# Four edits to an eight-image, four-layer kernel on one core: stores from two queues, an input sum by rows, a constant from DRAM, a longer loop body

## The chip, the core and the metric

One core of a Trainium2 chip. The time is the device time of one execution in microseconds (us). Eight images of 16 channels and 128 x 128 pixels in float32 go through four layers; the 128 partitions hold image and channel, 16,384 columns the pixels.

## What is computed

Each layer adds to x its function of the group-normed x (`_gn`: mean and variance over pairs of channels). Cut to what matters:

```python
x = x + L0(gn(x))   # attention over the 3 rows of a 3x3 patch, 48 features, 4 heads, MLP with gelu; sum, 1x1 convolution, bias
x = x + L1(gn(x))   # out1 = mean, out3 = max over the image; out = W4 (x (1 + sigmoid(tanh(wh)) + sigmoid(tanh(gray))))
x = x + L2(gn(x))   # sum over 3x3 taps and channels of P/Q, P = polynomial of degree 5, Q = 1 + |polynomial of degree 4|
x = x + L3(gn(x))   # 3x3 convolution of silu(x) and of 8 cubic splines of x, bias
```

## The kernel before

The four layers run one after the other, each in blocks in which every engine has its own stream of instructions, with semaphores between them. A block ends when all streams have ended.

**Layer 0** (`layer0`) works in 64 chunks (`NCHUNKS`), each 8 image columns of 2 images. A round `n` runs four stages for four chunks: centring of chunk n, the heads of chunk n - 1, the attention of chunk n - 2, the MLP of chunk n - 3. `steps` (lines 179 to 187) gives each engine its rounds: the first 3 written out, then a loop `Fori` of (63 - 3) / 4 = 15 passes with a body of `TURNS` = 4 rounds, then the last 4 written out. PE, VectorE, ScalarE and GpSimd use it; SyncE's stream is written out whole. In each round ScalarE takes one exponential of the softmax (line 693).

**Layer 1** (`layer1`) loads x and the eight pieces of layer 0's result x1, which lies by columns (w outer, h inner). VectorE adds x, x1 and a bias piece by piece (line 827, a piece is 16 image columns) and takes four bn_stats of it (line 99); the semaphore `x_in[j]` says that a piece is there, `xb_in` that x and the bias are. After `Norm` come the maximum of each partition over the whole image (line 835), the folding of weights, and a loop of 16 tiles of 1024 columns (tanh gates). The result goes to `x2` in four stores, and normed and with edges of zeros to the tile `GP` (16,797 columns).

**Powers** (`powers`) takes `GP` in 21 chunks of 800 columns (the last 797). ScalarE and VectorE make the powers 1 to 5, and of each a high, a middle and a low part in bf16 (`hi`, `mid`, `lo`, three buffers each). SyncE stores each part of a chunk to `pw` in DRAM, 1000 KB a store, in runs of 1600 bytes; before ScalarE writes `hi` and VectorE `lo` of chunk k, they wait until the stores of chunk k - 3 have landed:

```python
if k >= BUF:
    act.wait_ge(stored[u], k // BUF * STORES)
```

After chunk 1 SyncE also loads the weights `wst` (9 loads).

**Layer 2** (`layer2`) reads `pw` in 33 x 2 = 66 pieces of 2036 columns ("supertiles"), each by 24 loads of 20 rows into one of three slots of `mv`. Three rows of `mv` are ones; VectorE sets all of `mv` to 1.0 slot by slot before the first loads (line 1328), and SyncE loads slot g after memset g + 1 (line 1184). TensorE waits for `c_in` (the small matrices `sums` and `pick`, loaded first of all) and for the 24 loads of a slot, then multiplies. Every other engine works on what TensorE makes.

**Layer 3** (`layer3`) is not touched. It has the only transfers that GpSimd issues before the change: loads `l_s<-g` of 64 partitions (lines 1619 to 1623).

In the traces, buffer prefixes are cut: `l_x` is X of layer 1, `l_g` G or GP of layer 1, `l_mv` is `mv`.

Of the kernel before, what the change touches and what calls it, by code (L numbers as in the profile page):

```python
# [11 lines left out]
P = 128  # L12
# [6 lines left out]
PW = W + 1  # L19
# [21 lines left out]
WCOLS = (NCG * (len(AROUND) // 2) + NCG) * 128  # L41
RAW2 = (CG * DEG + 1) * 2 * WCOLS // 128
# [105 lines left out]
SLOTS0 = 2  # L148
BANK = 512
# [7 lines left out]
assert FS == 64 and 2 * HREST == P and SETS * FS == P and (LEAD_OUT - LEAD_IN) % TURNS == 0  # L157
# [561 lines left out]
def layer1(nc, x, x1, bias0, x2, pair, w1, raw2, pieces, wst, pw):  # L719
# [7 lines left out]
    with ExitStack() as ctx:  # L727
# [4 lines left out]
        with ExitStack() as ctx1:  # L732
# [14 lines left out]
            top = sb1("l1_top", [P, 8])  # L747
            stat = sb1("l1_stat", [P, 8])
# [12 lines left out]
            xb_in = sem("l1_xb_in")  # L761
# [8 lines left out]
            sum_done = sem("l1_sum_done")  # L770
# [4 lines left out]
            padded = sem("l1_padded")  # L775
# [5 lines left out]
            with nc.Block() as block:  # L781
                @block.sync
                def _(sp):
                    sp.dma_start(rest2[:], raw2).then_inc(raw_in, 16)
                    for k in range(LOADS):
                        n = HW // LOADS
                        if k == 0:
                            sp.dma_start(X[:], x).then_inc(xb_in, 16)
                            sp.dma_start(shift0[:], bias0).then_inc(xb_in, 16)
                        sp.dma_start(G[:, k * n:(k + 1) * n], x1[:, k * n:(k + 1) * n]).then_inc(x_in[k], 16)  # L790
# [12 lines left out]
                    sp.wait_ge(stored, 7 * 16)  # L803

                @block.vector
                def _(dve):
# [11 lines left out]
                    image, laid = X[:].rearrange("p (h w) -> p w h", w=W), G.rearrange("p (w h) -> p w h", h=H)  # L818

                    def chunk_in(e, k):  # L820
                        if k % (norm.CHUNKS // LOADS) == 0:
                            j = k // (norm.CHUNKS // LOADS)
                            at = slice(j * cols, (j + 1) * cols)
                            e.wait_ge(x_in[j], 16)
                            if j == 0:
                                e.wait_ge(xb_in, 32)
                            link(v.scalar_tensor_tensor(image[:, at, :], laid[:, at, :], shift0[:], image[:, at, :], ALU.add, ALU.add))

                    def chunk(k, n):
                        at = k * n // H  # L830
                        return image[:, at:at + n // H, :]
# [3 lines left out]
                    link(v.reduce_max(top[:, 0:1], X[:], AX.X))  # L835
# [19 lines left out]
                    for t in range(NT + 2):  # L855
# [4 lines left out]
                        if 1 <= t <= NT:  # L860
                            j = (t - 1) % 2
                            dve.wait_ge(gates_ready, t)
                            v.scalar_tensor_tensor(gate[:, j, 0, :], gate[:, j, 0, :], 4.0, gate[:, j, 1, :],
                                                   ALU.add, ALU.add).then_inc(sum_done, 1)
                            dve.wait_ge(sum_done, t)
# [3 lines left out]
                        if t >= 2:  # L869
                            dve.wait_ge(out_done, t - 1)  # L870
                            for q in range(2):
# [6 lines left out]
                                    ALU.mult, ALU.add).then_inc(padded, 1)  # L878

                @block.gpsimd  # L880
                def _(pool):
                    pool.wait_ge(norm2_ready, 1)
                    g = nc.gpsimd
                    g.memset(GP[:, 0:PW], 0.0).then_inc(padded, 1)
                    g.memset(GP[:, PW:PW + H * PW].rearrange("p (h w) -> p h w", w=PW)[:, :, 0:1], 0.0).then_inc(padded, 1)
                    g.memset(GP[:, PW + H * PW:IMG], 0.0).then_inc(padded, 1)
# [34 lines left out]
                def _(act):  # L921
# [3 lines left out]
                    for k in range(NT):  # L925
# [3 lines left out]
                        for m in range(2):  # L929
# [10 lines left out]
                                 scale=norm2.rstd[:]).then_inc(padded, 1)  # L940
# [3 lines left out]
def powers(nc, ctx, GP, pieces, wst, pw):  # L944
# [6 lines left out]
    STORES = 3 * 16  # L951
    with ExitStack() as ctx2:
# [17 lines left out]
        stored = [sem(f"pw_stored{u}") for u in range(BUF)]  # L970

# [5 lines left out]
        with nc.Block() as block:  # L977
            @block.sync
            def _(sp):
                lines = pw.rearrange("t c i (b n) -> t b c i n", b=NB)  # L980
# [12 lines left out]
                for u in range(BUF):  # L993
                    sp.wait_ge(stored[u], len(chunks[u::BUF]) * STORES)
# [29 lines left out]
            def _(act):  # L1024
                s = nc.scalar
                for k, (at, n) in enumerate(chunks):
# [7 lines left out]
                    if k >= BUF:  # L1034
                        act.wait_ge(stored[u], k // BUF * STORES)
# [45 lines left out]
def layer2(nc, pw, wst, l2w, planes, out2):  # L1081
# [8 lines left out]
    with ExitStack() as ctx:  # L1090
# [22 lines left out]
        mv_cleared = sem("l2_mv_cleared")  # L1113
# [29 lines left out]
        with nc.Block() as block:  # L1143
            @block.sync
            def _(sp):
                sp.dma_start(sums[:], l2w[0]).then_inc(c_in, 16)
                sp.dma_start(pick[:], l2w[1]).then_inc(c_in, 16)
# [83 lines left out]
            def _(pe):  # L1231
# [24 lines left out]
                pe.wait_ge(c_in, 32)  # L1256
# [519 lines left out]
def build(nc, io, stages=(0, 1, 2, 3)):  # L1776
# [7 lines left out]
    pw = dram("pw", (3, C, DEG, LINE), BF16)  # L1784
    pieces = dram("pieces", (3, CG * DEG + 1, 2 * WCOLS), BF16)
# [123 lines left out]
```

## Time and profile before

| | |
|---|---|
| median of 3 runs (lowest to highest) | 9925.01 us (9913.86 to 9939.9) |
| the profiled execution, its time | 9921.5 us |
| its span, first to last instruction | 9919.7 us |
| TensorE matmul busy | 8149.7 us (82%) |
| VectorE busy | 7774.4 us (78%) |
| ScalarE busy | 7513.9 us (76%) |
| GpSimd busy | 6175.0 us (62%) |
| SyncE's DMA queue (q1) | 536.51 MB |
| GpSimd's DMA queue (q0) | 17.87 MB |
| mean granted TensorE clock | 0.942 |

Busy shares are means over stages that differ. A stage is read in its own stretch: the timeline gives each operation's start, length and, in square brackets, the idle time of its engine before it and what ended it. Names like `SPq` mean the queue of the engine: the time in which it issues a transfer, not that in which the bytes move. "DMA share" is the mean busy share of the 16 DMA engines.

### The profile page before, as it was taken

How to read it: one execution, taken by the hardware profiler on the slowest of the kernel's cores; microseconds unless marked ns; L12 is line 12 of the kernel's file. 1: busy time of each engine (PE TensorE's matmuls, PEld its weight loads, DVE VectorE, ACT ScalarE, POOL GpSimd, SP SyncE). 2: the span in 40 equal slices, each digit the busy share in tenths (PEclk: the TensorE clock that was granted, in tenths of full speed). 3: DMA queues.
4: the chain of work that ended last, by engine and by line, in shares of the span. 5: the costliest groups of instructions: out<-in, count | busy, mean ns of one | idle time of the engine just before them, and what ended most of it. 6: DMA issues, size and time to landing. Idle time of an engine off the chain costs nothing. (4 is left out here: it accounts for less than half of the span.)

```text
span 9919.7 us, 141478 instructions
## 1 busy us (share of the span) xinstructions
PE 8149.7 (82%) x35038; PEld 2741.3 (28%) x35038; DVE 7774.4 (78%) x9339; ACT 7513.9 (76%) x8313; POOL 6175.0 (62%) x3353
## 2 busy tenths in 40 slices
PE   6999999999999995306888888888888888883689
PEld 2333333333333331101222222222222222220233
DVE  6777777777777776867888888888888888885777
ACT  4676666666666673557899989989889899893787
POOL 3555555555555552007888888888888888882111
PEclk9999999999999997658999999999999999996899
DMA  2000000000000001253323323223223223235555
GB/s 85 13 12 11 11 13 12 11 11 13 12 11 11 11 9 76 100 181 82 66 55 69 66 55 69 64 57 69 62 60 69 60 61 69 58 62 132 130 137 128
DMA packets 258450, 565.42 MB, mean 57 GB/s; under 512 B 71660, under 2 KB 179788, under 8 KB 244184
## 3 DMA queue, kind: packets, MB, share of 16 engines
q1 hardware_dynamic: 221746, 536.51, 22.2%
q0 software_dynamic: 35744, 17.87, 1.0%
q8 instruction: 388, 6.36, 0.3%
q14 instruction: 572, 4.68, 0.2%
HBM read 367.15 MB, written 186.72 MB: 56 GB/s over the span
## 5 line engine op out<-in xcount | busy, mean ns | idle before, releaser
L1226 POOL TENSOR_TENSOR l_a<-l_a 128x1018 f32<-128x1018 f32 x2116 | 3923.1, 1885 | 581.7 <-ACT l_a L1389 569.5
L1351 DVE TENSOR_TENSOR l_r<-l_pps,l_a 128x509 f32<-128x509 f32 x4232 | 2641.8, 680 | 640.2 <-PE l_pps L1239 640.1
L1389 ACT ACTIVATE l_a<-l_a 128x2036 f32<-128x2036 f32 x1193 | 2269.9, 1903 | 116.3 <-DVE l_a L1357 94.0
L1239 PE MATMUL l_qps<-l_mv,wst 123*128 123x509 bf16 x4246 | 1317.7, 393 | 722.9 <-DMA l_mv<-pw 408.3
L1382 ACT ACTIVATE l_a<-l_qps 128x1018 f32<-128x1018 f32 x1592 | 1592.3, 1019 | 380.0 <-PE l_qps L1239 370.8
L599 POOL TENSOR_TENSOR a_pr<-a_pr 128x768 f32<-128x768 f32 x384 | 896.6, 2335 | 811.1 <-DVE a_pr L537 795.2
L1239 PE MATMUL l_pps<-l_mv,wst 123*128 123x509 bf16 x4232 | 1348.0, 389 | 9.8 <-DVE l_r L1351 1.5
L675 ACT ACTIVATE a_g<-a_fps 128x512 f32<-128x512 f32 x1152 | 645.8, 596 | 757.5 <-PE a_fps L419 632.1
L1292 PE MATMUL l_aux<-l_r,l_sums 128*32 128x509 f32 x8448 | 1131.0, 607 | 51.0 <-DVE l_o L1335 30.2
L1357 DVE TENSOR_SCALAR l_a<-l_qps 128x1018 int32<-128x1018 int32 x796 | 961.0, 1207 | 9.3 <-PE l_qps L1239 8.0
L537 DVE TENSOR_TENSOR a_pr<-a_qkv,a_at 128x768 f32<-128x768 f32 x576 | 854.8, 1537 | 2.2
L426 PE MATMUL a_cps<-a_g,a_wfp 128*64 128x512 f32 (+1 forms) x2304 | 823.9, 629 | 0.7 <-ACT a_g L675 0.7
L1239 PEld LDWEIGHTS l_qps<-l_mv,wst 123*128 123x128 bf16 x4246 | 300.3, 99 | 1858.7 <-issue 946.0
L654 ACT ACTIVATE a_r<-a_tps,a_eps 128x512 f32<-128x512 f32 (+1 forms) x960 | 625.1, 672 | 184.5 <-PE a_tps L379 135.0
L605 POOL TENSOR_TENSOR a_h<-a_tc,a_r 128x512 f32<-128x512 f32 (+1 forms) x192 | 205.3, 1097 | 838.8 <-ACT a_r L654 838.8
L548 DVE TENSOR_TENSOR a_x<-a_cps,a_x 128x512 f32<-128x512 f32 x384 | 257.4, 682 | 541.5 <-PE a_cps L426 541.5
L1239 PEld LDWEIGHTS l_pps<-l_mv,wst 123*128 123x128 bf16 x4232 | 420.3, 99 | 770.6 <-DVE l_r L1351 373.7
L419 PE MATMUL a_fps<-a_h,a_wfc 128*128 128x512 f32 x768 | 440.7, 656 | 104.0 <-ACT a_g L675 104.0
L413 PE MATMUL a_fps<-a_h,a_wfc 48*128 48x512 f32 x1536 | 444.2, 655 | 92.7 <-ACT a_g L675 49.8
L609 POOL TENSOR_TENSOR a_r<-a_x,a_r 128x1024 f32<-128x1024 f32 x192 | 454.6, 2400 | 95.1 <-ACT a_r L654 95.1
L541 DVE TENSOR_TENSOR a_h<-a_x,a_r 128x512 f32<-128x512 f32 x384 | 448.3, 1208 | 79.8 <-ACT a_r L654 59.7
L1619 POOL DMA_DIRECT2D l_s<-g x66 | 45.9, 696 | 683.9 <-DMA l_s<-g 435.2
(180 smaller groups left out, 11931.8 us busy)
## 6 DMA issues: line engine op xcount, KB each, us to landing
l_mv<-pw SPq DMA_DIRECT2D x1608, 79.5 KB
l_gx<-g SPq DMA_DIRECT2D x66, 1040.0 KB
l_sh<-planes SPq DMA_DIRECT2D x536, 127.2 KB, 6.7
planes<-l_s SPq DMA_DIRECT2D x66, 1018.0 KB, 4.6
a_xt<-g SPq DMA_DIRECT2D x192, 160.0 KB, 3.3
pw<-pw_hi SPq DMA_DIRECT2D x20, 1000.0 KB
pw<-pw_mid SPq DMA_DIRECT2D x20, 1000.0 KB
pw<-pw_lo SPq DMA_DIRECT2D x20, 1000.0 KB
```

Of the source, the lines that this page charges most:

```text
L426: last = t_.matmul(cps[lo * FS:hi * FS, c % 2, :], flat(wfp[:, m, lo:hi, :]), G[:, g % 2, m, :], start=m == 1, stop=m == 2, skip_group_che ...
L537: v.tensor_tensor(out, val, a, ALU.mult).then_inc(val_v, 1)
L599: g_.tensor_tensor(y, y, PR[:, 3 * e + d, :], ALU.add).then_inc(val_p, 1)
L654: s_.activation(r, of, ACT.Abs_reciprocal_sqrt, bias=eps[:], scale=1.0 / EMB).then_inc(t_read, 1)
L675: s_.activation(G[:, g % 2, m, :], fps[:, bank % 2, :], ACT.Gelu).then_inc(f_read, 1)
L1226: g.tensor_tensor(a, a, a, ALU.mult).then_inc(sq_p, 1)
L1239: return t.matmul(out, wst[:, k, n * P:(n + 1) * P], x[:, n // NPP, cols], start=True, stop=True)
L1292: last = t.matmul(aux[32 * pp:32 * pp + 32, 0:SUB], sums[:, 0, :], R[:, NPP * k + pp, :], start=k == 0, stop=k == NCG - 1, skip_group_chec ...
L1351: v.tensor_tensor(to, pps[:, (2 * m + h) % P_BANKS, 0:SUB], pair_of(A, m)[:, h, :], ALU.mult).then_inc(mul_done, 1)
L1357: v.tensor_scalar(pair_of(A, s).bitcast(I32), q.bitcast(I32), 0x7FFFFFFF, None, ALU.bitwise_and).then_inc(abs_v, 1)
L1382: s_.activation(pair_of(A, s), q, ACT.Abs).then_inc(abs_a, 1)
L1389: s_.activation(a, a, ACT.Abs_reciprocal_sqrt, bias=1.0).then_inc(root_done, GROUP)
```

## The change

1. `powers`: the stores are split over two queues. SyncE stores `hi` of every chunk and `lo` of odd chunks; GpSimd stores `mid` of every chunk and `lo` of even ones, with semaphores `stored_p` of its own. Who waits for a buffer waits for both queues.
2. `layer1`: the sum of x, x1 and bias goes through a piece row by row (128 rows of 16 columns) in place of column by column, so do the bn_stats, and a piece's maximum over each row of 16 (`tops`) is taken right behind the sum; the maximum over the image is taken of these 1024 values.
3. `layer2`: the three memsets of `mv` are gone. GpSimd sets a tile of 48 x 509 ones in layer 1, SyncE stores it to DRAM (`ones`) there, and in layer 2 loads three rows of it into each slot behind the slot's 24 loads. `sums` and `pick` are loaded behind slot 0. TensorE waits for all five.
4. `steps`: the body of layer 0's loop has `ROUNDS` = 12 rounds, with 5 passes.
5. Semaphores: `xb_in` is merged into `x_in[0]`, `sum_done` into the chain, `padded`, for which nobody waited, is dropped.

```diff
+ROUNDS = 12
...
-    with engine.Fori(0, (LEAD_OUT - LEAD_IN) // TURNS) as thrice:
-        for i in range(TURNS):
-            body(Plan(thrice * TURNS + (LEAD_IN + i), (LEAD_IN + i) % TURNS, LEAD_IN))
+    with engine.Fori(0, (LEAD_OUT - LEAD_IN) // ROUNDS) as again:
+        for i in range(ROUNDS):
+            body(Plan(again * ROUNDS + (LEAD_IN + i), (LEAD_IN + i) % TURNS, LEAD_IN))
...
+                    sp.wait_ge(one_made, 1)
+                    sp.dma_start(ones.rearrange("r n -> (r n)").rearrange("(p n) -> p n", p=ONES), one[:]).then_inc(stored, 16)
...
-                    image, laid = X[:].rearrange("p (h w) -> p w h", w=W), G.rearrange("p (w h) -> p w h", h=H)
+                    image, laid = X[:].rearrange("p (h w) -> p h w", w=W), G.rearrange("p (w h) -> p h w", h=H)
...
-                            e.wait_ge(x_in[j], 16)
-                            if j == 0:
-                                e.wait_ge(xb_in, 32)
-                            link(v.scalar_tensor_tensor(image[:, at, :], laid[:, at, :], shift0[:], image[:, at, :], ALU.add, ALU.add))
+                            e.wait_ge(x_in[j], 16 if j else 48)
+                            link(v.scalar_tensor_tensor(image[:, :, at], laid[:, :, at], shift0[:], image[:, :, at], ALU.add, ALU.add))
+                            v.tensor_reduce(tops[:, j, :], image[:, :, at], AX.X, ALU.max)
...
-                    link(v.reduce_max(top[:, 0:1], X[:], AX.X))
+                    link(v.reduce_max(top[:, 0:1], tops[:].rearrange("p k h -> p (k h)"), AX.X))
...
+        def wait_stored(e, k):
+            e.wait_ge(stored[k % BUF], by_sp(k))
+            e.wait_ge(stored_p[k % BUF], by_pool(k))
...
-                    for m, (t, ready) in enumerate(((hi, hi_ready), (mid, mid_ready), (lo, lo_ready))):
-                        sp.wait_ge(ready, (k + 1) * DEG)
-                        sp.dma_start(lines[m, :, :, :, at:at + n], t[:, k % BUF, :, 0:n]).then_inc(stored[k % BUF], 16)
+                    sp.wait_ge(hi_ready, (k + 1) * DEG)
+                    sp.dma_start(lines[0, :, :, :, at:at + n], hi[:, k % BUF, :, 0:n]).then_inc(stored[k % BUF], 16)
+                    if k % 2:
+                        sp.wait_ge(lo_ready, (k + 1) * DEG)
+                        sp.dma_start(lines[2, :, :, :, at:at + n], lo[:, k % BUF, :, 0:n]).then_inc(stored[k % BUF], 16)
...
+            @block.gpsimd
+            def _(pool):
+                for k, (at, n) in enumerate(chunks):
+                    pool.wait_ge(mid_ready, (k + 1) * DEG)
+                    nc.gpsimd.dma_start(lines[1, :, :, :, at:at + n], mid[:, k % BUF, :, 0:n]).then_inc(stored_p[k % BUF], 16)
+                    if k % 2 == 0:
+                        pool.wait_ge(lo_ready, (k + 1) * DEG)
+                        nc.gpsimd.dma_start(lines[2, :, :, :, at:at + n], lo[:, k % BUF, :, 0:n]).then_inc(stored_p[k % BUF], 16)
...
-                        dve.wait_ge(stored[k % BUF], k // BUF * STORES)
+                        wait_stored(dve, k - BUF)
...
-                        act.wait_ge(stored[u], k // BUF * STORES)
+                        wait_stored(act, k - BUF)
...
                 for g in range(SLOTS):
-                    sp.wait_ge(mv_cleared, g + 1)
                     load_supertile(g, g)
+                    sp.dma_start(mv[KROWS - 3:KROWS, g].rearrange("p c n -> p (c n)"), ones).then_inc(c_in, 16)
+                    if g == 0:
+                        sp.dma_start(sums[:], l2w[0]).then_inc(c_in, 16)
+                        sp.dma_start(pick[:], l2w[1]).then_inc(c_in, 16)
...
-                pe.wait_ge(c_in, 32)
+                pe.wait_ge(c_in, 80)
...
-                for u in range(SLOTS):
-                    v.memset(mv[:, u], 1.0).then_inc(mv_cleared, 1)
```

SyncE's queue at the beginning of the powers, before and then after the change:

```order
L984 DMA pw<-pw_hi 8x80x800
L984 DMA pw<-pw_mid 8x80x800
L984 DMA pw<-pw_lo 8x80x800
L984 DMA pw<-pw_hi 8x80x800
L984 DMA pw<-pw_mid 8x80x800
L984 DMA pw<-pw_lo 8x80x800
L988 DMA wst<-pieces 20x5120 x6
L991 DMA wst<-pieces 1x5120 x3
```

```order
L995 UNCONDITIONAL_BRANCH
L999 DMA pw<-pw_hi 8x80x800 x2
L1002 DMA pw<-pw_lo 8x80x800
L1006 DMA wst<-pieces 20x5120 x6
L1009 DMA wst<-pieces 1x5120 x3
L999 DMA pw<-pw_hi 8x80x800 x2
L1002 DMA pw<-pw_lo 8x80x800
```

and GpSimd's queue there now (before, it had nothing between the edges of `GP` and layer 2):

```order
L1014 UNCONDITIONAL_BRANCH
L1018 DMA pw<-pw_mid 8x80x800
L1021 DMA pw<-pw_lo 8x80x800
L1018 DMA pw<-pw_mid 8x80x800 x2
L1021 DMA pw<-pw_lo 8x80x800
L1018 DMA pw<-pw_mid 8x80x800 x2
```

Of the three stores of a chunk SyncE keeps one or two, and GpSimd issues the others. (The outermost count of a store is 8, images; then 80 powers of channels, and 800 columns.)

SyncE's queue at the start of layer 2, before and after:

```order
L1144 UNCONDITIONAL_BRANCH
L1146 DMA l_sums<-in_w_sums 128x64
L1147 DMA l_pick<-in_w_pick 128x32
L1159 DMA l_mv<-pw 20x2036 x72
L1189 DMA planes<-l_sh 128x2036
L1189 DMA planes<-l_sh 128x256 x2
```

```order
L1170 UNCONDITIONAL_BRANCH
L1183 DMA l_mv<-pw 20x2036 x24
L1208 DMA l_mv<-ones 3x8144
L1210 DMA l_sums<-in_w_sums 128x64
L1211 DMA l_pick<-in_w_pick 128x32
L1183 DMA l_mv<-pw 20x2036 x24
L1208 DMA l_mv<-ones 3x8144
L1183 DMA l_mv<-pw 20x2036 x24
L1208 DMA l_mv<-ones 3x8144
L1216 DMA planes<-l_sh 128x2036
L1216 DMA planes<-l_sh 128x256 x2
```

The small matrices go behind slot 0's loads, and three loads of ones are added, one behind each slot's 24.

VectorE in layer 1, the last pieces before, and the first two after (there are eight):

```order
L99 BN_STATS n_stats<-l_x 128x6 x4
L827 SCALAR_TENSOR_TENSOR l_x<-l_g,l_shift,l_x 128x16x128
L99 BN_STATS n_stats<-l_x 128x6 x4
L106 BN_AGGR n_own<-n_stats 128x2
L107 COPY n_spread<-n_own 128x1
```

```order
L829 SCALAR_TENSOR_TENSOR l_x<-l_g,l_shift,l_x 128x128x16
L830 TENSOR_REDUCE l_tops<-l_x 128x128
L100 BN_STATS n_stats<-l_x 128x6 x4
L829 SCALAR_TENSOR_TENSOR l_x<-l_g,l_shift,l_x 128x128x16
L830 TENSOR_REDUCE l_tops<-l_x 128x128
L100 BN_STATS n_stats<-l_x 128x6 x4
```

The sum runs over 128 rows of 16 columns in place of 16 columns of 128 rows, and each piece has a maximum of its own.

## Rows read from the trace of the kernel before

**Rows 1.** Stretches: length, PE, PEld, DVE, ACT, POOL busy, clock, DMA share, GB/s.

```profile
50.00:3882.00 3832.00, 3524.31 (x10516) 1382.25 (x10516) 2821.89 (x2827) 2584.50 (x4225) 2109.97 (x1024) 0.98 0.06 12
...
4116.00:4493.00 377.00, 0.00 (x0) 0.00 (x0) 229.54 (x253) 198.13 (x252) 0.12 (x1) 0.50 0.52 175
```

**Rows 2.** Timeline of ScalarE, layer 0: start, us, engine, line, operation.

```profile
157.52 0.68 ACT L693 ACTIVATE a_at<-a_at 128x576 f32<-128x576 f32 x1
...
330.08 0.68 ACT L693 ACTIVATE a_at<-a_at 128x576 f32<-128x576 f32 x1
...
391.73 0.68 ACT L693 ACTIVATE a_at<-a_at 128x576 f32<-128x576 f32 x1
...
3672.00 0.68 ACT L693 ACTIVATE a_at<-a_at 128x576 f32<-128x576 f32 x1
```

**Rows 3.** Line 183, layer 0's loop: ns min/median/max, first and last start.

```profile
L183 PEldq COMPARE_BRANCH  x15: 83/3770/3869, 380.3 to 3664.7; - x15
```

**Rows 4.** Timeline of VectorE, layer 1's input.

```profile
3908.65 4.69 DVE L827 SCALAR_TENSOR_TENSOR l_x<-l_g,l_shift,l_x 128x2048 f32<-128x2048 f32 x1 [18.78 <-DMA l_g<-x]
...
3972.00 3.75 DVE L99 BATCH_NORM_STATS2 n_stats<-l_x 128x6 f32<-128x512 f32 x4
...
3980.04 17.21 DVE L835 TENSOR_REDUCE l_top<-l_x 128x1 f32<-128x16384 f32 x1
```

**Rows 5.** Timeline of the powers, in the middle of the stage.

```profile
4324.96 5.59 SPq L984 DMA_DIRECT2D pw<-pw_hi  x1
...
4424.32 0.87 ACT L1041 ACTIVATE pw_hi<-l_g 128x800 bf16<-128x800 f32 x1 [7.73 <-DMA pw<-pw_lo]
...
4427.30 5.60 SPq L984 DMA_DIRECT2D pw<-pw_hi  x1
```

**Rows 6.** Timeline, the powers' first chunks and layer 2's first issue.

```profile
4117.55 1.89 DVE L1016 TENSOR_TENSOR pw_up<-pw_up,l_g 128x800 f32<-128x800 f32 x2 [1.20 <-ACT pw_up L1031]
...
4122.25 0.77 SPq L984 DMA_DIRECT2D pw<-pw_hi  x1
...
4161.35 1.88 DVE L1016 TENSOR_TENSOR pw_up<-pw_up,l_g 128x800 f32<-128x800 f32 x2
...
4492.88 0.37 SPq L1146 DMA_DIRECT2D l_sums<-in_w_sums  x1
```

**Rows 7.** Busy time in stretches: powers, layer 2's first loads, layer 3's stores of `g`.

```profile
4200.00:4440.00 240.00, 0.00 (x0) 0.00 (x0) 152.75 (x168) 130.73 (x168) 0.00 (x0) 0.50 0.53 181
...
4501.00:4529.00 28.00, 6.39 (x14) 1.24 (x14) 16.71 (x5) 8.78 (x7) 3.49 (x2) 0.56 0.61 137
...
9150.00:9160.00 10.00, 0.00 (x0) 0.00 (x0) 3.21 (x3) 0.00 (x0) 0.00 (x0) 0.50 0.93 268
```

**Rows 8.** VectorE by line and form (layer 1; norm before layer 0), and its timeline.

```profile
L863 DVE SCALAR_TENSOR_TENSOR l_gate<-l_gate 128x1024 f32<-128x1024 f32 x16 | 19.4, 1215 | 8.7 <-ACT l_gate L935 8.7
...
L99 DVE BATCH_NORM_STATS2 n_stats<-n_x 128x6 f32<-128x512 f32 x32 | 19.4, 678 | 7.3 <-DMA n_x<-in_x 7.2
...
3765.90 4.78 DVE L510 TENSOR_REDUCE a_sc<-a_pr 128x72 f32<-128x864 f32 x5
```

**Rows 9.** Timeline of GpSimd and VectorE in layer 3.

```profile
9222.86 2.33 DVE L1695 TENSOR_TENSOR l_bases<-l_vb,l_na 128x2080 f32<-128x2080 f32 x1
9222.94 0.67 POOL L1620 DMA_DIRECT2D l_s<-g  x1
...
9224.87 1.73 POOL L1620 DMA_DIRECT2D l_s<-g  x1
9225.11 1.24 DVE L1674 TENSOR_SCALAR l_vb<-l_vb 128x2080 f32<-128x2080 f32 x1
```

**Rows 10.** Timeline, layer 2's start, and the landing times of line 1189's stores.

```profile
4501.61 27.23 SPq L1159 DMA_DIRECT2D l_mv<-pw  x72
...
4517.89 1.86 PE L1239 MATMUL l_qps<-l_mv,wst 123*128 123x509 bf16 x4 [408.29 <-DMA l_mv<-pw]
...
DMA to landing us min/median/max: 1.7/1.8/17.7
```

More of the change, by code:

```diff
@@ L156 @@
 LEAD_IN, LEAD_OUT = 3, NCHUNKS - 1
-assert FS == 64 and 2 * HREST == P and SETS * FS == P and (LEAD_OUT - LEAD_IN) % TURNS == 0
+assert FS == 64 and 2 * HREST == P and SETS * FS == P and ROUNDS % TURNS == 0 and (LEAD_OUT - LEAD_IN) % ROUNDS == 0
 class Plan:
@@ L717, in _, with layer1 @@
                 steps(act, body)
-def layer1(nc, x, x1, bias0, x2, pair, w1, raw2, pieces, wst, pw):
+def layer1(nc, x, x1, bias0, x2, pair, w1, raw2, pieces, ones, wst, pw):
     TILE = 1024
@@ L747, in layer1 @@
             top = sb1("l1_top", [P, 8])
+            tops = sb1("l1_tops", [P, LOADS, H])
+            one = sb1("l1_one", [ONES, SUB], BF16)
             stat = sb1("l1_stat", [P, 8])
@@ L862, in _ @@
                             dve.wait_ge(gates_ready, t)
-                            v.scalar_tensor_tensor(gate[:, j, 0, :], gate[:, j, 0, :], 4.0, gate[:, j, 1, :],
-                                                   ALU.add, ALU.add).then_inc(sum_done, 1)
-                            dve.wait_ge(sum_done, t)
+                            link(v.scalar_tensor_tensor(gate[:, j, 0, :], gate[:, j, 0, :], 4.0, gate[:, j, 1, :],
+                                                        ALU.add, ALU.add))
                             v.tensor_tensor(gate[:, j, 0, :], gate[:, j, 0, :], tile(G, t - 1), ALU.mult).then_inc(mix_ready, 1)
@@ L877, in _ @@
                     v.tensor_scalar(rows[:, 0:DVE_ROWS], image[:, 0:DVE_ROWS], norm2.rstd[:], norm2.shift[:],
-                                    ALU.mult, ALU.add).then_inc(padded, 1)
+                                    ALU.mult, ALU.add)
                 @block.gpsimd
                 def _(pool):
+                    g = nc.gpsimd
+                    g.memset(one[:], 1.0).then_inc(one_made, 1)
                     pool.wait_ge(norm2_ready, 1)
[L883 to L886, printed above, removed]
+                    g.memset(GP[:, 0:PW], 0.0)
+                    g.memset(GP[:, PW:PW + H * PW].rearrange("p (h w) -> p h w", w=PW)[:, :, 0:1], 0.0)
+                    g.memset(GP[:, PW + H * PW:IMG], 0.0)
                 @block.tensor
@@ L939, in _ @@
                     s.activation(rows[:, DVE_ROWS:H], image[:, DVE_ROWS:H], ACT.Identity, bias=norm2.shift[:],
-                                 scale=norm2.rstd[:]).then_inc(padded, 1)
+                                 scale=norm2.rstd[:])
         powers(nc, ctx, GP, pieces, wst, pw)
@@ L970, in powers, with by_sp, by_pool @@
         stored = [sem(f"pw_stored{u}") for u in range(BUF)]
+        stored_p = [sem(f"pw_stored_p{u}") for u in range(BUF)]
+        def by_sp(k):
+            return sum(1 + j % 2 for j in range(k % BUF, k + 1, BUF)) * 16
+        def by_pool(k):
+            return sum(2 - j % 2 for j in range(k % BUF, k + 1, BUF)) * 16
+        def wait_stored(e, k):
+            e.wait_ge(stored[k % BUF], by_sp(k))
+            e.wait_ge(stored_p[k % BUF], by_pool(k))
+        lines = pw.rearrange("t c i (b n) -> t b c i n", b=NB)
         def power(k, i):
@@ L992, in _ @@
                 sp.wait_ge(wst_in, (len(A_PARTS) + 3) * 16)
-                for u in range(BUF):
-                    sp.wait_ge(stored[u], len(chunks[u::BUF]) * STORES)
+                for k in range(len(chunks) - BUF, len(chunks)):
+                    wait_stored(sp, k)
+            @block.gpsimd
[6 more added lines that the diff above has]
+                        nc.gpsimd.dma_start(lines[2, :, :, :, at:at + n], lo[:, k % BUF, :, 0:n]).then_inc(stored_p[k % BUF], 16)
             @block.vector
@@ L1079, in among, with layer2 @@
     return (s // CYCLE) * len(members) + sum(n <= s % CYCLE for n in members)
-def layer2(nc, pw, wst, l2w, planes, out2):
+def layer2(nc, pw, wst, ones, l2w, planes, out2):
     everyone = set(range(CYCLE))
@@ L1784, in build @@
     pw = dram("pw", (3, C, DEG, LINE), BF16)
+    ones = dram("ones", (3, NCG * SUP), BF16)
     pieces = dram("pieces", (3, CG * DEG + 1, 2 * WCOLS), BF16)
@@ L1795, in build @@
         if 1 in stages:
-            layer1(nc, x, x1, io["w0_bias"], x2, io["pair"], (io["w1_mats"], io["w1_vecs"]), io["w2_raw"], pieces, wst, pw)
+            layer1(nc, x, x1, io["w0_bias"], x2, io["pair"], (io["w1_mats"], io["w1_vecs"]), io["w2_raw"], pieces, ones, wst, pw)
         if 2 in stages:
-            layer2(nc, pw, wst, (io["w2_sums"], io["w2_pick"]), planes, out2)
+            layer2(nc, pw, wst, ones, (io["w2_sums"], io["w2_pick"]), planes, out2)
     if 3 in stages:
```

21 lines of the change are left out of this document (8 added, 13 removed).

## The prediction

> **What bounds the kernel now.** I read the stages first [rows 1]: layer 0 takes 3832 us, the powers of layer 1 377 us, with VectorE busy for 230 us of those and ScalarE for 198. The change touches four places, so I read each for the wait that ends last there.
>
> Layer 0's loop, by the softmax's exponential, one per round on ScalarE [rows 2]. The 60 rounds between the loop's first and last take 3672.00 - 157.52 = 3514.5 us. A round inside a body is (330.08 - 157.52) / 3 = 57.52 us, and 60 of them are 3451.2. The other 63 us lie in the rounds behind a branch back: 391.73 - 330.08 = 61.65, 4.1 more. Of 14 such rounds the extra is 2.1 to 5.4 us, 61 in all, 4.4 on average; 2 us lie elsewhere. TensorE's branch itself takes 3.77 us at the median [rows 3], and in it no matmul of the next body is issued.
>
> Layer 1's input, on VectorE [rows 4]: eight pieces, each one addition of x, x1 and the bias and four bn_stats, from 3908.65 to 3972.00 + 3.75 = 3975.75, that is 67.1 us or 8.4 a piece; then the small matmuls of the norm, then a maximum over all 16,384 columns, 17.21 us, with the gates waiting behind it. 84.3 us in the two.
>
> Powers: a chunk takes (4427.30 - 4324.96) / 6 = 17.06 us, SyncE's queue is issuing all of it (5.6 to 5.7 us a store, three a chunk), and ScalarE waits 7.7 us a chunk for the store of the lowest part three chunks back [rows 5]. Before the buffers fill, VectorE starts a chunk every (4161.35 - 4117.55) / 4 = 10.95 us [rows 6]. So the stores bind. What in them does? While they run the DMA engines are busy 0.53 of the time; the stores of layer 3 from 32 partitions reach 0.93, and layer 2's loads of 20 rows 0.61 [rows 7]. These shares are near 8, 16 and 10 of 16, and the store's outermost count is 8 (8x80x800), the others' 32 and 20. I read it so: a store of the powers uses half of the engines, and that half is full. The Trainium skill says the same (DMA: Bandwidth & Descriptors, section "Why a DMA increments its semaphore by 16 and not by 1"): the count is the largest up to 16 that divides both outermost sizes. The trace agrees, 0.53 being 8.5 of 16.
>
> **The change, part by part.** The sum is made against the profiled execution, 9921.5 us (1.8 outside its span of 9919.7); the median of the runs is 3.5 us more.
>
> Loop of twelve rounds. Five passes in place of 15, 4 branches back in place of 14. Nothing else moves in the order of any engine. 10 x 4.4 = **-44 us**. If a branch costs more with the longer body, 5.4 for each of the four remaining, it is 61 - 22 = -39; all at 2.1 of the ten, -21.
>
> Input sums by rows, maximum by pieces. The addition before steps by 512 bytes in x (read and write) and runs along x1; now it runs in stretches of 16 along x and steps in x1. Nearest rows [rows 8]: an operation of two inputs in a row takes 1.215 us for 1024 columns, 2.43 for 2048; bn_stats costs 3.75 / 4 = 0.94 us when it steps [rows 4] and 19.4 / 32 = 0.61 when it does not, so a stepped read costs 0.33 us on 512, 1.3 on 2048. That gives 3.7 us for the new addition; its bounds are 2.4 (no step felt) and 4.7 (as now). Four bn_stats now read in stretches: 2.5 us. The new maximum of a piece, 2048 columns in groups of 16: 4.78 us for 4224 columns in groups of 12 is 1.13 ns each, so 2.3 us. A piece is 8.5 us, eight are 68.0, the last maximum over 1024 values 1.1: 69.1 against 84.3, **-15 us** (-25 to -7). The eight pieces follow one another at 8.4 us now with no wait for x1 but the first's, and the new ones are no faster, so no load gets in the way.
>
> Ones from DRAM, the store: one memset of GpSimd, idle then, and one store on SyncE's queue ahead of the x2 stores, hidden by the gates. Zero; without that cover a store is some 2 us. The dropped semaphores cost nothing either: nobody waited for `padded`, and the link does what `sum_done` did.
>
> Powers' stores. Of 63 stores SyncE keeps 31 (every hi, every other lo), GpSimd issues 32. A store keeps one half of the engines full for 17.06 / 3 = 5.69 us. What the change gives hangs on where GpSimd's stores go. If on the same half, the rate stays: 17.06. If all on the other half, VectorE is next: 10.95. If evenly on all sixteen, the first half has 1.5 + 0.75 stores a chunk, 12.8 us. No row of this trace shows it (the only transfers GpSimd issues are layer 3's loads, of 64 partitions). I take the even spread, between the ends, and keep both. Then the first half works 31 x 5.69 + 16 x 5.69 = 267 us, the load of `wst` 7, and with some 3 at the start before it is full and 2 of landing 279 us from the first store at 4122.25, so to 4401. Now layer 2's first issue is at 4492.88 [rows 6], and the stores end some 2 us ahead of it, at 4490: **-89 us** (0 to -130, the latter with the last lows at 4117.6 + 21 x 10.95 + 4.7 = 4352 and 8 us for the last store). The same section of that page of the Trainium skill has what GpSimd issues go either to its count of engines by a cursor that moves round, or to all 16; both would give 12.8.
>
> GpSimd also has to make these transfers: a load of 64 rows takes it 0.67 us [rows 9]; a store has 640 rows, so between 0.67 and 6.7 us. At 6.7 it is 10 us a chunk, below 12.8. Behind its waits nothing is queued on GpSimd but its next stores; the waits of ScalarE and VectorE for a buffer now ask for both queues.
>
> Start of layer 2. VectorE's three memsets go, and with them SyncE's wait: loads start at 4492.9 instead of 4501.6, 8.7 us sooner. But TensorE now waits for five transfers in `c_in`, and the fifth is the ones row of the third slot, behind all 72 loads. Before, it started when slot 0 had landed: 4517.89, 25.0 us after the queue's first issue [rows 6, 10]. The 72 loads were issued in 27.2 us but moved slower: the store right behind them, issued at 4528.9, took 17.7 to land, at 4546.6; its own 1.04 MB are 3.9 us at the 268 GB/s of layer 3's stores [rows 7], so all loads had moved by 4543, 41 us after the first issue. With some 4 for the five small ones and landing (an estimate), TensorE starts 45 us after the first issue: **+20 us**. If the ones did not queue behind the loads' data but only behind their issue, it is 72 x 0.378 + 2 + 2 = 31.4, so +6. TensorE has nothing else to do, and everything in layer 2 follows it, so this is on the path whole.
>
> Sum: -44 - 15 - 89 + 20 = -128, so 9921.5 - 128 = 9793.5; with the median's offset about **9796 us**.
>
> **Rivals.**
> *VectorE binds the powers* (GpSimd's stores on free engines). For it: half of the engines idle at 0.53, and the first four chunks did run at 10.95. Against: nothing says that GpSimd's go only there. -44 - 15 - 130 + 20 = -169: 9755.
>
> *The engines stay as full as they were* (GpSimd's stores on the same half, or a byte rate near 180 GB/s that is the memory's for rows of 1600 bytes). For it: 181 GB/s in every window of the stage [rows 7]. Against: 268 GB/s with rows of 2080 bytes. Powers between 15 and 17 us: 9885 at 17, 9843 at 15.
>
> *GpSimd is too slow*, and the kernel is slower. Its descriptors are made by the engine itself. In layer 3 one issue took 1.73 instead of 0.67 us, ending as a TENSOR_SCALAR of VectorE ended (9225.11 + 1.24 = 9226.4) [rows 9]. Were 640 rows to cost 6.7 us free and 2.6 times that beside VectorE, a store would take 17 us, a chunk 26, the powers 21 x 9 = 190 us more than now: -39 + 190, about 10,075. The kernel is slower than before from a chunk of 17.06 + 39 / 21 = 18.9 us, a store of 12.6 on GpSimd. Against: an issue beside TENSOR_TENSOR (9222.86 to 9225.2) took its 0.67 us, and the powers have only TENSOR_TENSOR on VectorE. The Trainium skill has this as a rule (SBUF — State Buffer, "Who interferes with whom"): making descriptors is locked out by two-port VectorE operations and not by tensor_tensor. By that section this rival falls; by the same page's summary of rules, which says to use the queues of SyncE or ScalarE under a VectorE operation, the change would be this loss.
>
> *The loop gives nothing*, where every pass refetches as much code as it does now in smaller pieces: 9840. Against: the extra sits only behind branches [rows 2].
>
> **How the numbers follow.** Even spread 0.47, VectorE binds 0.18, engines as full as before 0.20, GpSimd too slow 0.07, the loop without gain or another mishap 0.08. The range takes 9738 (the second with some of the layer 1 and layer 2 bounds) to 9874 (the third at all but its end). A measurement of this kernel tells about 0.3%, 30 us. Faster by more than that 0.89: all but the fourth and mixtures; same 0.04; slower 0.07.
>
> **What would show it.** The exponential's rounds with four long ones left, 4.4 us each. VectorE's piece at 8.5 us and no 17 us maximum. In the powers a chunk of 12.8 us, ScalarE still waiting some 2 us for a store, the DMA share at 0.7 or above; 10.95 and no wait, or 17 with an unchanged share, names the rival. GpSimd's store issues below 7 us. TensorE's first matmul of layer 2 some 45 us after SyncE's first issue there. Wrong altogether: a chunk over 18.9 us, or layer 2's rounds changed, which nothing here touches.

## The result and the profile after

The changed kernel takes 9870.29 us (median of four, 9866.99 to 9893.29), the kernel before, run beside it, 9932.45: a ratio of 0.9944, 95% interval 0.9921 to 0.9967. That is 62 us, where 128 were forecast. The profiled execution took 9893.29, span 9891.4.

Stages of the changed kernel: length, PE, PEld, DVE, ACT and POOL busy, clock, DMA share, GB/s (answers to [rows 1, 7]; the first three are layer 0's loop, the powers, and their middle).

```profile
50.00:3838.00 3788.00, 3500.57 (x10516) 1372.30 (x10516) 2822.49 (x2827) 2586.86 (x4226) 2110.17 (x1025) 0.99 0.06 12
4056.00:4387.00 331.00, 0.00 (x0) 0.00 (x0) 229.27 (x252) 200.15 (x252) 38.97 (x32) 0.50 0.72 199
4100.00:4340.00 240.00, 0.00 (x0) 0.00 (x0) 171.34 (x189) 148.33 (x188) 27.92 (x23) 0.50 0.74 205
...
4438.90:8951.00 4512.10, 3898.42 (x20606) 1089.60 (x20606) 3843.04 (x5619) 4062.71 (x3379) 3922.85 (x2116) 0.98 0.29 61
8951.00:9891.00 940.00, 634.63 (x3704) 229.37 (x3704) 634.71 (x411) 591.67 (x403) 132.58 (x203) 0.83 0.56 137
```

The last two are layers 2 and 3, which nobody edited. Before, the same stretches are these:

```profile
4517.90:9006.00 4488.10, 3895.73 (x20606) 1087.54 (x20606) 3840.01 (x5619) 4061.45 (x3378) 3923.11 (x2116) 0.98 0.29 63
9006.00:9919.00 913.00, 632.84 (x3704) 230.28 (x3704) 635.21 (x412) 592.41 (x404) 135.43 (x203) 0.84 0.57 141
```

Layer 2 is 24 us longer at the same busy times, layer 3 27 us. Both are taken up below. The two profiled executions thus differ by 28 us only (spans 9891.4 and 9919.7); the profiled one of the changed kernel is the slowest of its four, 23 us above their median.

Timeline of ScalarE and layer 0's branch on TensorE (answers to [rows 2, 3]):

```profile
155.58 0.68 ACT L695 ACTIVATE a_at<-a_at 128x576 f32<-128x576 f32 x1
...
3625.80 0.69 ACT L695 ACTIVATE a_at<-a_at 128x576 f32<-128x576 f32 x1
...
L185 PEldq COMPARE_BRANCH  x5: 83/3702/3764, 838.6 to 3618.5; - x5
```

The 60 rounds take 3470.2 us, 44.3 less, and four of them are long.

Timeline of VectorE, layer 1's input (answers to [rows 4]); the second and the last piece, and the last maximum:

```profile
3872.38 3.67 DVE L829 SCALAR_TENSOR_TENSOR l_x<-l_g,l_shift,l_x 128x2048 f32<-128x2048 f32 x1
3876.08 2.29 DVE L830 TENSOR_REDUCE l_tops<-l_x 128x128 f32<-128x2048 f32 x1
3878.28 2.46 DVE L100 BATCH_NORM_STATS2 n_stats<-l_x 128x6 f32<-128x512 f32 x4
...
3934.76 1.22 DVE L839 TENSOR_REDUCE l_top<-l_tops 128x1 f32<-128x1024 f32 x1
```

From 3864.07 to 3935.98 it is 71.9 us, where 3908.65 to 3997.25 was 88.6: 16.7 less.

Timeline of the powers (answers to [rows 5, 6]), then the landing times of the middle part's stores on GpSimd's queue:

```profile
4061.61 0.78 SPq L999 DMA_DIRECT2D pw<-pw_hi  x1
...
4125.61 0.85 ACT L1071 ACTIVATE pw_mid<-l_g 128x800 bf16<-128x800 f32 x1
...
4236.68 29.86 SPq L999 DMA_DIRECT2D pw<-pw_hi  x2
...
4266.51 0.87 ACT L1068 ACTIVATE pw_hi<-l_g 128x800 bf16<-128x800 f32 x1 [17.63 <-DMA pw<-pw_lo]
...
4337.83 0.86 ACT L1071 ACTIVATE pw_mid<-l_g 128x800 bf16<-128x800 f32 x1
...
L1018 POOL DMA_DIRECT2D pw<-pw_mid x21: 1213/1213/1347, 4065.7 to 4365.8; - x21
...
DMA to landing us min/median/max: 11.0/14.8/21.7
```

Between the two `pw_mid` rows lie 14 chunks: 212.22 / 14 = 15.16 us each, not 12.8. They are uneven, 9.3 to 28.5 us, and the long ones end with a wait for a store, above all the lowest part's of an odd chunk, on SyncE's queue. From the first store at 4061.61 to layer 2's first issue at 4387.38 are 325.8 us, against 370.6 before. GpSimd's issue takes 1.21 us, so its queue is not slow to issue.

Timeline of layer 2's start (answers to [rows 10]):

```profile
4387.38 8.89 SPq L1183 DMA_DIRECT2D l_mv<-pw  x24
...
4416.82 0.40 SPq L1208 DMA_DIRECT2D l_mv<-ones  x1
...
4438.93 1.88 PE L1266 MATMUL l_qps<-l_mv,wst 123*128 123x509 bf16 x4 [389.97 <-DMA l_mv<-ones]
```

TensorE starts 51.55 us after the first issue and 22 us after the third row of ones was issued; before it was 25.0.

### The profile page after: what moved, and what is told of

Its sections match the earlier page's. It is cut to its first block and busy times, and to the rows that moved or that the text cites. A ratio compares the mean times of both kernels' runs of the same rounds, so it can differ in the third digit from the quotient of the medians.

```text
span 9891.4 us, 141423 instructions
## 1 busy us (share of the span) xinstructions
PE 8131.2 (82%) x35038; PEld 2732.7 (28%) x35038; DVE 7741.1 (78%) x9344; ACT 7517.6 (76%) x8313; POOL 6211.1 (63%) x3386
```

## The experiments

Each comparison is with the kernel before, run beside it. Stage times are from the profiled execution of each.

**The loop alone.** The kernel before with `ROUNDS = 12` and the loop of the change.

> The kernel before with the loop of twelve rounds as its only change. Theory: the loop's part of the change stands alone and is -44 us (the exponential's rounds 3 to 63 take 3470 us in place of 3514.5, with four long ones left), so about 9888 where before is 9932. The other half of the question is layer 2, whose ten rounds behind a branch back are 74.0 us in the changed kernel and 72.5 before: if the longer program of layer 0 moves layer 2's code to where a refetch costs more, they are 74 here too and 15 us of the 44 are given back; if that was one execution's chance, they are 72.5. Layer 3 885 us as before, or 913 as in the changed kernel's profiled execution.

9881.03 us against 9925.76, ratio 0.995 (0.9937 to 0.9964): 45 us. The 60 rounds of the loop take 3469.7 us where those of before took 3514.5. Layer 2's rounds behind a branch are 72.64 us, 72.5 before, so the longer loop costs next to nothing there. Layer 3, counted from the last store of `planes`, took 943.6 us where before has 913.0, with no edit near it (the expectation counts both from its first load, 28 us later).

**The powers' stores back on SyncE.** The changed kernel with

```
-                    sp.wait_ge(hi_ready, (k + 1) * DEG)
-                    sp.dma_start(lines[0, ...], hi[...])
-                    if k % 2:
-                        sp.wait_ge(lo_ready, (k + 1) * DEG)
-                        sp.dma_start(lines[2, ...], lo[...])
+                    for m, (t, ready) in enumerate(((hi, hi_ready), (mid, mid_ready), (lo, lo_ready))):
+                        sp.wait_ge(ready, (k + 1) * DEG)
+                        sp.dma_start(lines[m, ...], t[...])
```

and no GpSimd block in the powers (arguments cut to `...`, here and below).

> The changed kernel with the powers' stores back on SyncE's queue, as before. Powers from the first store to layer 2's first issue 370 us again, 17.06 a chunk, so 45 us more than the changed kernel: about 9915 from its median of 9870. Layer 2 would then start as late after its first issue as in the changed kernel, 51 us, or sooner (45) if the stores' tail on GpSimd's queue was what slowed the first loads.

9895.16 us, ratio 0.9963 (0.9948 to 0.9977). The stage is 370.6 us again, 45 more than in the changed kernel, and yet the time is only 25 us more: layer 2 is 4492.6 us here and 4512.1 there. So the split gives 45 us in its stage and costs some 20 in layer 2, by the two traces; of the whole times the intervals overlap, and 25 us between medians taken beside different runs is a rough figure. The start of layer 2 stays at 52.8: no tail of GpSimd's stores slows it.

**All stores on GpSimd.** The changed kernel with hi, mid and lo in GpSimd's block, none on SyncE.

> The changed kernel with all 63 stores of the powers on GpSimd's queue and none on SyncE's. Theory A (what binds is two queues on the same engines: GpSimd's stores go to all sixteen and, in packets of 4800 bytes, push SyncE's aside on the eight they share, which lie half idle at other times): with one queue on all sixteen at 0.21 us a packet of 4800 bytes, 366 GB/s, a store is 2.8 us and VectorE binds, a chunk 11 us, the stage some 75 us shorter than the 325.8 of the changed kernel. Theory B (a byte rate common to all, the 209 GB/s seen while GpSimd's store had 14 to 16 engines to itself): 4.9 us a store, 14.7 a chunk, the stage as in the changed kernel or slower. Theory C (what binds is the wait for the odd chunk's lowest part, which SyncE issues last, and not the engines): that wait is gone and the chunk is 11 us as in A, but the engines' rate while a store runs would be no higher than now.

9797.76 us, ratio 0.988 (0.986 to 0.990). The stage is 254.0 us, the chunk 10.95, VectorE's own pace, so theory B (14.7) falls. The queues of the two kernels in the stretch 4125 to 4270 (packets, MB, share of 16 engines' time), the changed one first:

```profile
q0 software_dynamic: 6476, 15.30, 43.5%
q1 hardware_dynamic: 8912, 14.08, 30.1%
```

```profile
q0 software_dynamic: 16992, 39.06, 92.2%
```

GpSimd's queue alone keeps 14.8 engines busy and moves 270 GB/s, where SyncE's alone had 8.5 and 181. So the queue reaches all sixteen, as the forecast took it, but a single store does not. The first store of this kernel, alone in 4061.5 to 4063, keeps eight busy; from 4064 on, with a second one under way, all sixteen work:

```profile
q0 software_dynamic: 56, 0.27, 50.0%
```

```profile
4064.00:4067.00 3.00, 0.00 (x0) 0.00 (x0) 2.96 (x5) 3.00 (x4) 1.32 (x2) 0.50 0.98 288
```

Of the spreads that the forecast names, it is the one in which a store takes as many engines as its outermost count, eight, and the next store takes others.

What a MB costs in engine time: 0.922 x 16 x 145 / 39.06 = 55 us on GpSimd's queue alone, 0.435 x 16 x 145 / 15.30 = 66 beside SyncE's, and 50 for SyncE's there (47 alone: 0.53 x 16 x 240 / 43.4). Packets are 4800 bytes on GpSimd's queue, 1600 on SyncE's. If half of GpSimd's engine time lies on the eight engines that SyncE's stores use, these have 0.301 x 16 + 0.435 x 16 / 2 = 8.3 at work, as good as the 8.5 when SyncE's stores run alone: they are full. At 8.5, a chunk of 1.5 and 1.5 stores of 1.024 MB is 1.5 x 1.024 x (50 + 33) / 8.5 = 15.0 us, and 15.16 was measured. That is no test, since the prices come from the same stretch; it says that full engines and these prices account for the time.

Where does the higher price come from? Not from two queues on the same engines. In the changed kernel both queues run in 4083 to 4089 on 8.7 engines in all, and in 4127 to 4132 on all sixteen:

```profile
q0 software_dynamic: 236, 0.80, 39.9%
q1 hardware_dynamic: 176, 0.28, 14.5%
```

```profile
q0 software_dynamic: 234, 1.10, 90.0%
q1 hardware_dynamic: 112, 0.18, 10.4%
```

The first is 48 us a MB for GpSimd's packets (0.399 x 16 x 6 / 0.80) and 50 for SyncE's, hardly more than SyncE's 47 alone; in the second GpSimd's cost 65. In steps of 1 us from 4125 to 4270 (a packet's bytes spread evenly over its time), 34 of the 145 us have both queues at work with fewer than 9.5 engines busy (3.6 and 4.3 on average), at 49 and 48 us a MB and 165 GB/s; 59 us have 14 or more busy, at 71 and 52 us and some 240 GB/s. The trace does not name the engines. That the 34 us are a GpSimd store on SyncE's own half, with the other half idle, is read from the sum near eight while SyncE's queue has stores waiting. So here a store is dearer when all sixteen engines work, and sixteen move 240 to 275 GB/s, less than twice the 181 of eight. Why is open.

Theories A and C each had 11 us here. C also had a rate no higher than in the changed kernel, which 270 GB/s against 203 speaks against; the next two runs test it once more.

**One store in three, one in six, on SyncE.**

```
-                    if k % 2:
-                        sp.wait_ge(lo_ready, (k + 1) * DEG)
-                        sp.dma_start(lines[2, ...], lo[...])
```

with lo of every chunk on GpSimd; and the same with hi of the even chunks on GpSimd too.

> The changed kernel with only the highest part's stores on SyncE's queue, both others on GpSimd's. Theory A (engines): GpSimd's two stores take 2.05 MB / 209 GB/s = 9.8 us, in which SyncE's gets 46 GB/s, 0.45 MB; its rest of 0.57 MB takes 3.2 us at 181: 13.0 us a chunk, the stage near 300 us. Theory C (the wait for the odd chunk's lowest part behind SyncE's next stores): no lowest part is on SyncE's queue any more, the wait is gone and VectorE binds: 11 us a chunk, 254 us.

> The changed kernel with one store of six on SyncE's queue (the highest part of odd chunks), the rest on GpSimd's. Theory A' (the eight engines that both use are the bound; a store of SyncE takes 6.1 us of them beside the other queue, one of GpSimd 3.9): 0.5 x 6.1 + 2.5 x 3.9 = 12.8 us a chunk. Theory D (whenever the two queues run together, everything moves at some 205 GB/s, whatever the split): 15 us as with 1.5 and with 1 of three, here shorter only where GpSimd's is alone. The kernel with all stores on GpSimd's queue took 10.95 to 12.8.

The first: 9862.83 us, stage 323.2, chunk 14.88. Theory A as written (13.0) and theory C (11) both miss: with no lowest part on SyncE's queue, ScalarE waits for its highest part instead. The second: 9857.48 us, stage 304.7, chunk 13.57 at 226 GB/s. Their queues, 4125 to 4270 and 4130 to 4330:

```profile
q0 software_dynamic: 8927, 20.16, 59.1%
q1 hardware_dynamic: 6503, 10.27, 22.9%
```

```profile
q0 software_dynamic: 16225, 37.15, 71.8%
q1 hardware_dynamic: 5049, 7.98, 14.4%
```

By the prices of the changed kernel a GpSimd store takes some 4.0 us of the shared engines, in place of 2.85, and one of SyncE 6.0, in place of 5.69. Carried over, that gives 14.0 and 12.9 us, 0.9 and 0.6 below what was measured; the second run's expectation had 12.8. Theory D (some 205 GB/s whenever both queues run) holds for the first, with 210 GB/s, and leaves room below 15 in the second without a number for it. The first account is within 7% of both, the second names no figure for the latter, and these runs do not decide between them. The rate rose with GpSimd's share of the stores, 203, 210 and 226 GB/s, to 270 with all of them.

**SyncE's stores on sixteen engines.** A store cut in eight, one for each block `b`, of 16 partitions:

```
-                        sp.dma_start(lines[0, :, :, :, at:at + n], hi[:, k % BUF, :, 0:n])
+                        for b in range(NB):
+                            sp.dma_start(lines[0, b, :, :, at:at + n], hi[b * C:b * C + C, k % BUF, :, 0:n])
```

once for hi and lo of every chunk with mid on GpSimd, once for all three on SyncE.

> The changed kernel with the stores of the highest and the lowest part on SyncE's queue as eight transfers of 16 partitions each, so that their outermost count is 16 and not 8, and the middle part's store on GpSimd's queue. What of the pace is the half of the engines that SyncE's transfers leave idle? Theory A (the pace is GpSimd's stores at some 209 GB/s, while SyncE's hardly move, and then SyncE's rest on its eight engines at 181): with SyncE's on sixteen too, no engine idles, all bytes go at the 266 GB/s of the run with one queue on sixteen engines, 3.07 MB a chunk in 11.5 us, and the stage takes some 255 to 265 us from its first store. Rival (two queues on the same engines hinder each other whatever the spread): the rate stays near 205 GB/s, the chunk at 15 us.

> All stores of the powers on SyncE's queue, in transfers of 16 partitions: 24 issues a chunk. If the outermost count alone decides how many engines a transfer uses and idle engines were what was lost, the DMA engines' share rises above 0.53 and what binds is the issuing, 24 x 0.61 = 14.6 us a chunk. If a queue of SyncE had but eight engines whatever the count, 17.06 a chunk and a share of 0.53. If, as the run with the middle part on GpSimd's queue suggests, a packet of such a transfer takes 0.13 us and not 0.075, the share rises to 0.9 and the rate stays at 180 to 190 GB/s: 16 to 17 us a chunk, no gain from the idle half.

The first: 9932.11 us, no gain on the kernel before (1.0009, 0.9996 to 1.0022), the stage 370.7 us and 17.2 a chunk at some 180 GB/s, so both theories miss, A's 255 to 265 us by over 100. The second, a single execution: 9857.29, the stage 347.5 us, 16.23 a chunk. Its stretch 4150 to 4300:

```profile
4150.00:4300.00 150.00, 0.00 (x0) 0.00 (x0) 102.01 (x114) 87.81 (x114) 0.00 (x0) 0.50 0.90 190
...
q1 hardware_dynamic: 21299, 28.41, 90.1%
```

The outermost count does decide how many engines work, as the Trainium skill says (DMA: Bandwidth & Descriptors, section "Why a DMA increments its semaphore by 16 and not by 1"); the trace agrees, 0.53 having become 0.90. But the rate rose from 181 to 190 GB/s only, since a packet of 1600 bytes took 0.120 us and not 0.075. For stores of this shape the idle half was worth 23 us of 370.6. These transfers also read 16 partitions each, so whether packet size or the few partitions slow them stays open.

**The ones first.**

```
                 for g in range(SLOTS):
+                    sp.dma_start(mv[KROWS - 3:KROWS, g]..., ones).then_inc(c_in, 16)
+                sp.dma_start(sums[:], l2w[0]).then_inc(c_in, 16)
+                sp.dma_start(pick[:], l2w[1]).then_inc(c_in, 16)
+                for g in range(SLOTS):
                     load_supertile(g, g)
-                    sp.dma_start(mv[KROWS - 3:KROWS, g]..., ones).then_inc(c_in, 16)
-                    if g == 0:
-                        sp.dma_start(sums[:], l2w[0]).then_inc(c_in, 16)
-                        sp.dma_start(pick[:], l2w[1]).then_inc(c_in, 16)
```

> The changed kernel with the three rows of ones, the sums and the pick issued ahead of layer 2's 72 loads. Theory: TensorE waits at its start for the ones row of the third slot, behind all 72 loads. Then its first matmul comes 18 to 20 us after SyncE's first issue and not 51.55, and the kernel is 32 us shorter, 9838. Rival: the first slot's loads land late too because 72 loads share the engines, and the start stays above 35 us: 9855 or more.

9835.73 us, ratio 0.9913 (0.9898 to 0.9927). The start (the view ends before the last 5 of the 72 loads):

```profile
4380.14 0.88 SPq L1207 DMA_DIRECT2D l_mv<-ones  x3
...
4381.94 28.03 SPq L1183 DMA_DIRECT2D l_mv<-pw  x67
...
4404.18 1.86 PE L1266 MATMUL l_qps<-l_mv,wst 123*128 123x509 bf16 x4 [362.10 <-DMA l_mv<-pw]
```

24.0 us after the first issue: 27.5 less. TensorE now waits for the first slot's loads. The 18 to 20 expected were too few by 4 to 6.

**Both.** All stores on GpSimd, the ones first.

> All the powers' stores on GpSimd's queue and the ones rows first in layer 2: the two gains add where they are apart, 72 + 28 us less than the changed kernel, so 9797.8 - 28 = 9770 at the median. Where the layer 2 start is slowed by GpSimd's last store still landing, the second gain is smaller, and the start is above 24 us after the first issue.

9768.38 us, ratio 0.9843 (0.9824 to 0.9861), the lowest median here: 102 us less than the changed kernel. The start is at 24.0. The powers took 272.8 us in this execution and 254.0 in the other with the same code: VectorE's pace asks for 3.07 MB in 10.95 us, 280 GB/s, and the queue gives 243 here on average (4062 to 4330) and 270 in the other's steady part, so it now and then falls behind.

**Waits in ScalarE's program.** Why is layer 2 longer in the changed kernel? Its rounds behind a branch back (ten of 66) took 74.0 us, before 72.5. Groups of ScalarE's square root from 4700 to 8700, before and changed (the last columns: idle before, and what ended it):

```profile
L1389 ACT ACTIVATE l_a<-l_a 128x2036 f32<-128x2036 f32 x1062 | 2020.7, 1903 | 104.4 <-DVE l_a L1357 84.6 <-ACT l_a L1382 19.9
```

```profile
L1414 ACT ACTIVATE l_a<-l_a 128x2036 f32<-128x2036 f32 x1055 | 2007.2, 1903 | 139.7 <-DVE l_a L1382 87.7 <-issue 32.2 <-ACT l_a L1407 19.7
```

"issue" is idle time that no semaphore ends: 32 us that before has none of, some 3.8 us at one place behind each branch. The split gives ScalarE a second semaphore to wait for in 18 chunks, which is one more instruction each ahead of layer 2: 8454 executed, against 8436 in the kernel with the stores back on SyncE. (The kernel before executes 8456, 20 of them for its ten further branches back in layer 0, so its program is not the longer one.) So the kernel with both improvements got 18 waits that are long met:

```
                     if k >= BUF:
+                        act.wait_ge(mid_ready, (k - BUF + 1) * DEG)
                         wait_stored(act, k - BUF)
```

then two such waits, then four.

> As the kernel with all stores on GpSimd's queue and the ones first, with one more wait, long met, in ScalarE's program in each of the 18 chunks from the fourth on (the split queues gave it one more wait there too). Theory: what makes layer 2's rounds behind a branch 74 us in both kernels with split queues and 72.6 in the four others is that ScalarE's program is 18 instructions longer ahead of layer 2, so that its loop lies elsewhere in memory and its refetch ends later: the branch rounds are 74 us here, 15 us in all, and the powers are unchanged. Rival: it is the two queues themselves, or another engine's program, and the rounds stay at 72.6.

> As the kernel with 18 further waits in ScalarE's program, with 36. If each instruction shifts the loop's place in memory and the refetch behind a branch depends on it, layer 2's branch rounds are neither 72.6 nor 74.5 by rule; 18 more may cost more, or fall back to 72.6. If the cost grew with the number of waits itself, they would be 76.5, and layer 2 60 us longer.

> The run with two further waits a chunk had the same 8454 instructions on ScalarE ahead of layer 2 as the run with one, since one wait instruction holds two waits, so it tested nothing new. Here four further waits, all long met, make two more instructions a chunk: 36, and 8472. Theory (place in memory): the cost behind a branch depends on where the loop lies, so at 36 it is another value again, and 72.6 or less is as possible as more. Rival (length): twice the cost, 76.5 a branch round. Rival (the kind of wait on pw_hi itself): 74.5 as with 18.

One: 9799.95 us, branch rounds 74.55, layer 2 4519.1 us against 4486.1: twice the 15 us expected. The ten rounds have 20 of the 33 us; the rest lies in the 55 others, 0.25 us each, but these differ by up to 0.17 us between kernels without the 18 instructions too, so it can't all be put down to them. Two: 9779.04, again 8454 instructions and again 74.48. Four: 8472 instructions, 9777.14 us, branch rounds 72.76, layer 2 4491.4. The same group for one and for four:

```profile
L1407 ACT ACTIVATE l_a<-l_a 128x2036 f32<-128x2036 f32 x1054 | 2006.7, 1904 | 138.7 <-DVE l_a L1375 86.5 <-issue 32.4 <-ACT l_a L1400 19.7
```

```profile
L1410 ACT ACTIVATE l_a<-l_a 128x2036 f32<-128x2036 f32 x1061 | 2018.9, 1903 | 104.9 <-DVE l_a L1378 85.0 <-ACT l_a L1403 19.9
```

With 18 instructions more the idle time is there, with 36 it is gone, and a queue or a store has no part in it. All seven kernels with 8454 instructions have branch rounds of 73.8 to 74.6 and a layer 2 of 4505 to 4519 us, the seven others 72.5 to 72.8 and 4486 to 4496. The medians of whole runs are too noisy to show it: the three kernels with added waits are 32, 11 and 9 us above the one without, in the order one, two, four. What the traces show is that the extra hangs on how many instructions lie ahead, not on the waits. That it is the loop's place in memory is the likely reading; no run looked at addresses.

**Layer 3.** It took 905.7 to 946.2 us over these profiled executions, with 913.0 before and 943.6 in the kernel with the loop alone. It is the same code. No kernel has two traces, so a spread between executions isn't seen directly, but the whole times speak for one: with the loop alone layer 3 was 31 us longer in the trace, in an execution 33 us above the median of its six, and that median is the full 45 us below the kernel before. The 27 us of the changed kernel's trace are read the same way, as no effect of the change; that is argued and not shown.

## Why the prediction was wrong

- **Loop, -44: right.** -44.3 in the trace and -45 by itself; four long rounds with an extra of 3.7 to 5.2.
- **Layer 1's input, -15: right.** -16.7. The addition took 3.67 for 3.7, the statistics 2.46 for 2.5, the maxima 2.29 for 2.3 and 1.22 for 1.1.
- **Ones from DRAM at nothing, the dropped semaphores at nothing: right;** the first store of the powers came 60.6 us earlier, the sum of the two terms above.
- **Powers, -89: wrong, -45.** The spread of GpSimd's queue over all sixteen engines was right (by halves in turn), and the stores still bind. The step that failed is "the first half has 1.5 + 0.75 stores a chunk, 12.8 us", which gives every store the 5.69 us of a half that it takes with the other half idle. With both halves at work that price does not hold: GpSimd's stores took 66 us of engine time a MB on average and SyncE's 50, against 47, which is a chunk of 15.2 us and 325.8 us in the stage. Why the price rises stays open.
- **GpSimd too slow: fell.** An issue of 640 rows took 1.21 us, near the lower end of 0.67 to 6.7, and never longer than 1.35 beside VectorE. VectorE has only TENSOR_TENSOR in this stage. The Trainium skill (SBUF — State Buffer, "Who interferes with whom") has that two-port operations of VectorE lock GpSimd out of making descriptors and tensor_tensor does not; the trace agrees. The row in the summary of that page of the Trainium skill, to use another queue under a VectorE operation, gives VectorE's 2x and 4x modes as its reason and is no argument against this change: all 63 stores on GpSimd's queue gave 72 us more.
- **Start of layer 2, +20: +26.5.** The mechanism was right. The loads drained slower than the estimate: a packet of 4072 bytes took 0.324 us against 0.279 before. Why is open; with all stores on SyncE's queue it took 0.329.
- **"Layer 2's rounds changed, which nothing here touches": wrong.** The second wait of ScalarE's chunks was looked at for what it waits for, and not for the instruction that it adds; it cost about 20 us.

Together: -44 - 17 - 45 + 26 + 20 = -60, beside -62 between the medians. The terms are from one trace each; the same two traces, with 24 us in layer 2 and 27 in layer 3, give -28, and so much do their spans differ. That the sum without layer 3 meets the medians rests on layer 3's 27 us being chance. The forecast fell short by 66 us; the terms give 68: 44 in the powers, 20 in layer 2's loop and 6 at its start, less 2 at the input. Two slips of the forecast's arithmetic weigh nothing: 9793.5 with the offset is 9797, and 72 x 0.378 + 2 + 2 is 31.2.

## What to carry to other kernels

A queue's share of busy engines is no measure of what is left: price transfers by engine time per MB in a stretch where as many engines work as will after the change, and try all of a stream on one queue before splitting it. A transfer that a start waits for belongs ahead of the bulk on its queue, since behind 72 loads it cost 27.5 us. Where an engine idles behind each branch back of a loop, look at its "issue" time after any edit ahead of it, on every engine.

## What was not expected of the hardware

- The same 640 rows of 1600 bytes go in packets of 4800 bytes from GpSimd's queue and of 1600 from SyncE's; the first alone moved 270 GB/s, the second 181 on 8.5 engines and 190 on 14.4.
- Two queues at work on some eight engines cost 49 and 48 us of engine time a MB, where one alone costs 47; with fourteen or more engines at work it was 71 and 52.
- 18 more instructions on ScalarE, in a stage of 260 us, made the layer after it 33 us longer in one trace, 20 of them behind its branches; 36 made it 5 us longer.
